# A tower over all pairs of 32 embeddings: split pair kernels streamed per half batch, against plain ones kept on chip in four stages

## What is computed

```python
p = emb_inputs[:, ROW]; q = emb_inputs[:, COL]          # 496 pairs
kp = jnp.einsum('bpj,ipj->bpi', p, kernel)              # kernel (64, 496, 64)
z = jnp.sum(kp * q, axis=-1)
h = jnp.concatenate([z, dense_ctx], axis=1)
h = jnp.maximum(h @ W_top1 + b_top1, 0.0)
h = jnp.maximum(h @ W_top2 + b_top2, 0.0)
y = h @ W_top3
```

## Time and profile before

| | us |
|---|---|
| runs | 574.8, 575.55, 579.02 (median 575.55) |
| the profiled execution | span 578.3; of the runs only 579.02 can hold it, 0.7 more |
| TensorE busy | 479.2 (83%) |
| VectorE busy | 368.1 (64%) |
| ScalarE busy | 120.6 (21%) |
| GpSimd (POOL) busy | 241.3 (42%) |
| DMA | 114.69 MB, mean 198 GB/s |

### The profile page before, as it was taken

How to read it: one execution, slowest core, us unless ns; L and a number is a source line. 1 busy time by engine, 2 the same in 40 slices (tenths; PEclk the granted TensorE clock), 3 DMA queues, 4 the chain that set the end, 5 groups by cost and what they waited for, 6 DMA issues and landing times.

```text
span 578.3 us, 6972 instructions
## 1 busy us (share of the span) xinstructions
PE 479.2 (83%) x2258; PEld 249.9 (43%) x2258; DVE 368.1 (64%) x361; ACT 120.6 (21%) x170; POOL 241.3 (42%) x243
## 2 busy tenths in 40 slices
PE   0568697888988979488998698689889889889998
PEld 0345353444444434244543354435444444445543
DVE  3667584667776855576730387576858787777720
ACT  3275212020121120011043140211212112011002
POOL 3887777776415514050057777764531000000000
PEclk9969897999898989798999799898989999998999
DMA  6768999999999899798886879999999989788600
GB/s 182 184 152 202 241 236 225 213 221 222 229 232 224 191 226 242 174 228 194 198 206 171 177 183 237 204 220 208 224 232 236 230 208 228 194 217 198 139 1 1
DMA packets 43927, 114.69 MB, mean 198 GB/s; under 512 B 9183, under 2 KB 9183, under 8 KB 43758
## 3 DMA queue, kind: packets, MB, share of 16 engines
q1 hardware_dynamic: 36136, 105.91, 78.8%
q0 software_dynamic: 7488, 7.75, 6.2%
q10 hardware_dynamic: 262, 0.52, 0.3%
HBM read 29.72 MB, written 0.00 MB: 51 GB/s over the span
## 4 chain that ended last, share of the span: by engine, by line
DMA 51%; SPq 26%; PE 17%; issue 4%; ACT 1%; DVE 0%; DVEq 0%; ACTq 0%
DMA kst<-ksplit 48%; SPq L290 17%; PE kp L672 6%; SPq L298 3%; PE kp L746 3%; DMA ksplit<-in_kd 3%; PE z_ps L689 3%; PE kp L754 2%; SPq L274 2%; SPq L317 1%; PE kp L715 1%; PE tr_ps L643 1%; DMA own<-split 1%; PE kp L760 1%; SPq L265 0%
## 5 line engine op out<-in xcount | busy, mean ns | idle before, releaser
L620 DVE TENSOR_TENSOR prod<-kp,pair 128x1024 f32<-128x1024 f32 x248 | 292.4, 1219 | 119.8 <-PE kp L672 119.5
L672 PE MATMUL kp<-own,kst 128*128 128x512 f32 x992 | 276.7, 423 | 62.4 <-DMA kst<-ksplit 49.2
L394 POOL DMA_INDIRECT raw<-in_tbl,ids_sb x232 | 239.0, 1030 | 190.8 <-PE tr_ps L643 106.0
L672 PEld LDWEIGHTS kp<-own,kst 128*128 128x128 f32 x992 | 186.4, 198 | 188.1 <-DVE prod L620 75.6
L689 PE MATMUL z_ps<-prod,ones_sel 128*32 128x512 f32 x992 | 139.2, 633 | 0.7 <-DVE prod L620 0.6
L438 ACT ACTIVATE ksplit<-ksplit 128x1024 fp32r<-128x1024 f32 x32 | 33.9, 1059 | 174.6 <-DMA ksplit<-in_kd 174.3
L443 ACT ACTIVATE pair<-tr_ps 128x512 f32<-128x512 f32 x29 | 17.3, 597 | 141.0 <-PE tr_ps L643 141.0
L558 DVE TENSOR_TENSOR ksplit<-ksplit 128x1024 fp32r<-128x1024 f32 x32 | 38.9, 1216 | 9.2 <-ACT ksplit L438 9.1
L564 DVE TENSOR_TENSOR split<-pair,split 128x512 fp32r<-128x512 f32 x29 | 20.2, 697 | 36.3 <-ACT split L447 35.9
L689 PEld LDWEIGHTS z_ps<-prod,ones_sel 128*32 128x32 f32 x992 | 20.1, 110 | 48.9 <-issue 39.2
L715 PE MATMUL kp<-own 125*128 125x512 f32 x48 | 16.6, 502 | 15.4 <-DVE own L592 15.0
(11 more groups left out here) (29 smaller groups left out, 50.3 us busy)
## 6 DMA issues: line engine op xcount, KB each, us to landing
kst<-ksplit SPq DMA_DIRECT2D x128, 512.0 KB
ksplit<-in_kd SPq DMA_DIRECT2D x32, 512.0 KB, 4.1
own<-split SPq DMA_DIRECT2D x116, 128.0 KB
raw<-in_tbl,ids_sb POOLq DMA_INDIRECT x232
pair<-pair SPq DMA_DIRECT2D x16, 128.0 KB
pair<-in_first_ids SPq DMA_DIRECT2D x6, 256.0 KB, 11.3
w_sb<-in_w SPq DMA_DIRECT2D x1, 1024.0 KB, 10.5
pair<-in_tbl SPq DMA_DIRECT2D x4, 250.0 KB
```

Of the source, the lines that this page charges most:

```text
L394: nc.gpsimd.indirect_dma_start(raw[:, k % RAW_RING, b, n, :], None, tables[f], bass.IndirectOffsetOnAxis(ap=ids_sb[:, col:col + 1], axis=0 ...
L620: nc.vector.tensor_tensor(prod[:, s % P_RING, :, :], kp[s % KP_RING][:, :, :], factor, ALU.mult).then_inc(prod_done, 1)
L672: last = nc.tensor.matmul(kp[s % KP_RING][:, q, :], kst[:, c % K_RING, part, t % 2, (t % CHUNK) // 2, :], own[:, o, :], start=(part == 0), ...
```

## The change

K stays unsplit and whole on the chip (`k_sb`, 124 slots x 128 x 128), loaded once during the first stage. The batch is taken in four stages of 256 rows. In a slot the owner of one tile is an even field and that of the other an odd one, so that the two products take rows 0 to 63 and 64 to 127 of the same `pair` place and of `k_sb`; each is a plain fp32 matmul over 64 rows x 256 columns, into its own PSUM bank. `own`, `split`, `kst` and `ksplit` are gone. A *unit* is two slots: 128 x 1024 numbers, 62 a stage, 248 in all. `prod` is a ring of 15 units.

Reductions come in batches of eight units (four in stage 0; the rest of a chunk is 6 or 2), behind the last but one unit of the next batch. Between two reductions lies a *run*. In each run of stages 1 to 3 ScalarE copies the second and the fourth unit's `kp` to `prod` (48 units in all, `SPILLED`); VectorE multiplies those in place, after the other units of the run. 24 units have more than one factor place and are multiplied by two instructions.

Groups are transposed in events: one group each in stage 0 and the first six of stage 1, then two. An event directly behind reductions (`by_halves`) is transposed in halves of 64 rows into the `kp` tile of a unit one or two ahead, which waits for the copy out. Gathers run `RAW_LEAD` = 5 groups ahead, the second of a two-group event also waits for a unit (`PACE`). A group has 256 rows, so four DMAs; 61 groups are gathered. The lookup by comparison stays for three groups of stage 0, in plain fp32. Nine matmuls on zeros stand at TensorE's start. All layers come at the end; the layers' weights are loaded into the places of K's first 24 slots. Everything is unrolled.

```diff
-KP_RING = 3 ... P_RING = 4 ... RAW_RING = 4 ... K_RING = 2 ... AHEAD = 4
+K_LOAD = 8
+K_AHEAD = 3
+KP_RING = 3
+PROD_RING = 15
+RAW_RING = 8
+RAW_LEAD = 5
+WIDTH = 256
+STAGES = ((1,) * GROUPS, (1,) * 6 + (2,) * 5, (2,) * 8, (2,) * 8)
+LAST = len(STAGES) - 1
+STAGES_PER_HALF = ROWS // WIDTH
+BATCH_UNITS = (8,) * 4
+FIRST_BATCH_UNITS = (4,) * 8
+LOOKUP = (0, 1, 2)
+SMALL, SMALL_C = 1000, 8
+HOT_PAUSE = 4
+HOT_UNITS = 2 * SMALL_C * WIDTH // (2 * ROWS)
+WARM = 9
+SPILL_AT = (1, 3)
+PACE = 6
+def summed_behind(b):
+    st, first, n = BATCHES[b + 1]
+    return first + (n - 2 if n % 4 == 0 else n - 1)
+def runs():
+    out = [[]]
+    for u in range(UNITS):
+        out[-1].append(u)
+        if BATCH_OF[u] and u == summed_behind(BATCH_OF[u] - 1):
+            out.append([])
+    return out
+def spilled_units():
+    return [run[i] for run in runs()[1:-1] for i in SPILL_AT if i + KP_RING < len(run)]
+SPILLED = spilled_units()
+DVE_ORDER = [u for run in runs() for u in [u for u in run if u not in SPILLED] + [u for u in run if u in SPILLED]]
 ...
+TRANSPOSE_AT = [0, 0, 0, 1, 2, 4, 7, 10, 13, 16, 19, 23, 27, 31, 35, 39, 43, 47, 51, 55, 59, 62, 65, 69, 77, 85, 93,
+                101, 109, 117, 124, 131, 139, 147, 155, 163, 171, 179, 186, 193, 201, 209, 217]
+def release_event(r):
+    return EVENT_OF[r - RAW_LEAD] if r >= RAW_LEAD else None
+def gather_unit(r):
+    e = release_event(r)
+    return TRANSPOSE_AT[e] + PACE if e is not None and release_event(r - 1) == e else 0
+def by_halves(e):
+    return len(EVENT[e][3]) > 0 and sums_before(TRANSPOSE_AT[e])
+def home_unit(e):
+    return TRANSPOSE_AT[e] + EVENT[e][2]
 ...
         def _(sp):
 ...
+            for u in range(UNITS):
+                st, s = UNIT[u]
+                for m in fours_at(u):
+                    mix_across(st, m)
+                if u == DENSE_AT:
+                    sp.wait_ge(kp_done, u + 1)
+                    sp.dma_start(z_sb[:, FC - 2:FC, :], dense).then_inc(dense_in, 16)
+                if st == 0 and s in K_LOAD_AT and K_LOAD_AT[s] + K_AHEAD < len(K_LOADS):
+                    sp.wait_ge(kp_done, u + 1)
+                    load_k(K_LOAD_AT[s] + K_AHEAD)
+                if st == LAST and s == W_SLOTS:
+                    sp.wait_ge(kp_done, u)
+                    sp.dma_start(w1_sb, w1).then_inc(weights_in, 16)
+                    sp.dma_start(w2_sb, w2).then_inc(weights_in, 16)
 ...
-            def gather(h, k):
 ...
+            for r, (g, b) in enumerate(GATHER):
+                if b and not GATHER[r - 1][1]:
+                    pool.wait_ge(ids_rest_in, 16)
+                if r >= RAW_LEAD:
+                    pool.wait_ge(transposed, release_event(r) + 1)
+                if gather_unit(r):
+                    pool.wait_ge(kp_done, gather_unit(r))
+                for i in range(2):
+                    for n in range(2):
+                        f = 2 * g + n
+                        nc.gpsimd.indirect_dma_start(
+                            raw[:, r % RAW_RING, i, n, :], None, tables[f],
+                            bass.IndirectOffsetOnAxis(ap=ids_sb[:, 2 * b + i, f:f + 1], axis=0),
+                        ).then_inc(raw_in[r % RAW_RING], 16)
         def _(act):
 ...
+            def evacuate(e):
+                st, k, n, raws = EVENT[e]
+                if st >= 2 and k == 0:
+                    act.wait_ge(prod_done, done_through(unit_at(st - 1, 0)))
+                act.wait_ge(transposed, e + 1)
+                to = pair[:, group_place(st, k):group_place(st, k) + n, :]
+                if by_halves(e):
+                    nc.scalar.activation(to.rearrange("p n w -> p (n w)").rearrange("p (m h c) -> p m h c", h=2, c=64),
+                                         halves_ps(e)[:, :, 0:2 * n * 64].rearrange("p h (m c) -> p m h c", c=64),
+                                         ACT.Copy).then_inc(evacuated, 1)
+                else:
+                    nc.scalar.activation(to, event_ps(e)[:, 0:n * WIDTH].rearrange("p (n w) -> p n w", n=n),
+                                         ACT.Copy).then_inc(evacuated, 1)
+            def spill(u):
+                act.wait_ge(reduced, BATCH_OF[u - PROD_RING] + 1)
+                act.wait_ge(kp_done, u + 1)
+                nc.scalar.activation(prod[:, u % PROD_RING, :, :], kp[u % KP_RING][:, :, :],
+                                     ACT.Copy).then_inc(spilled, 1)
 ...
         def _(dve):
 ...
+            def make_hot(i):
+                dve.wait_ge(hot_ids_in[i], 16)
+                for c in range(SMALL_C):
+                    if (i or c) and c % HOT_PAUSE == 0:
+                        dve.wait_ge(hot_ready, SMALL_C * i + c)
+                    nc.vector.tensor_scalar(hot(i, c), hot_ids_sb[:, i, :], row_sb[:, c:c + 1], None,
+                                            ALU.is_equal).then_inc(hot_ready, 1)
+            for u in DVE_ORDER:
+                if u >= PROD_RING and BATCH_OF[u - PROD_RING] >= summed:
+                    summed = BATCH_OF[u - PROD_RING] + 1
+                    dve.wait_ge(reduced, summed)
+                tiles = [tile for x in unit_slots(u) for tile in SLOT[x]]
+                if u in SPILLED:
+                    dve.wait_ge(spilled, SPILLED.index(u) + 1)
+                    columns = prod[:, u % PROD_RING, :, :]
+                else:
+                    dve.wait_ge(kp_done, u + 1)
+                    columns = kp[u % KP_RING]
+                if len({factor_place(st, tile) for tile in tiles}) == 1:
+                    wait_factors(st, tiles[:1])
+                    place = factor_place(st, tiles[0])
+                    nc.vector.tensor_tensor(
+                        prod[:, u % PROD_RING, :, :].rearrange("p q (i n) -> p (q i) n", i=UNIT_SLOTS),
+                        columns[:, :, :].rearrange("p q (i n) -> p (q i) n", i=UNIT_SLOTS),
+                        pair[:, place:place + 1, :].broadcast_to([P, 2 * UNIT_SLOTS, WIDTH]),
+                        ALU.mult).then_inc(prod_done, 1)
 ...
-                    for part in range(2):
-                        last = nc.tensor.matmul(kp[s % KP_RING][:, q, :],
-                                                kst[:, c % K_RING, part, t % 2, (t % CHUNK) // 2, :],
-                                                own[:, o, :], start=(part == 0), stop=(part == 1))
+            def transpose_event(e):
+                st, k, n, raws = EVENT[e]
+                if by_halves(e):
+                    pe.wait_ge(prod_done, DONE_AT[home_unit(e) - KP_RING])
+                elif e > 1:
+                    pe.wait_ge(evacuated, e if e > 2 else 1)
 ...
+                    pe.wait_ge(raw_in[r % RAW_RING], (r // RAW_RING + 1) * 4 * 16)
+                    for i in range(2):
+                        rows = raw[:, r % RAW_RING, i, :, :].rearrange("p a n -> p (a n)")
+                        if by_halves(e):
+                            to = ((g - k) * 2 + i) * 64
+                            for h in range(2):
+                                half = slice(64 * h, 64 * h + 64)
+                                last = nc.tensor.transpose(halves_ps(e)[:, h, to:to + 64], rows[half, :],
+                                                           ident[half, half])
+                        else:
+                            to = (g - k) * WIDTH + i * P
+                            last = nc.tensor.transpose(event_ps(e)[:, to:to + P], rows, ident[:, :])
+                last.then_inc(transposed, 1)
+            def products(u):
+                st, s = UNIT[u]
+                if u - KP_RING in SPILLED:
+                    pe.wait_ge(spilled, SPILLED.index(u - KP_RING) + 1)
+                elif u >= KP_RING:
+                    pe.wait_ge(prod_done, DONE_AT[u - KP_RING])
+                for e in range(len(EVENT)):
+                    if by_halves(e) and home_unit(e) == u:
+                        pe.wait_ge(evacuated, e + 1)
+                for i, x in enumerate(unit_slots(u)):
+                    if st == 0 and x in K_LOAD_AT:
+                        pe.wait_ge(k_in[K_LOAD_AT[x]], 16)
+                    for q in range(2):
+                        owner = SLOT[x][q][0]
+                        rows = slice(64 * q, 64 * q + 64)
+                        pe.wait_ge(evacuated, group_event(st, owner // 2) + 1)
+                        last = nc.tensor.matmul(kp[u % KP_RING][:, q, i * WIDTH:(i + 1) * WIDTH], k_sb[rows, x, :],
+                                                pair[rows, group_place(st, owner // 2), :],
+                                                start=True, stop=True)
+                last.then_inc(kp_done, 1)
+            def reductions(b):
+                st, first, n = BATCHES[b]
+                tiles = batch_tiles(b)
+                c = tiles[0][0] // CHUNK_UNITS
+                if tiles[0][0] == 0 and st:
+                    pe.wait_ge(z_last, st)
+                elif tiles[0][0] and tiles[0][0] % CHUNK_UNITS == 0:
```

(85 more changed lines are left out.)

832 lines of the change are left out of this document (308 added, 524 removed).

## The result

The changed kernel takes 427.03 us (426.82 to 428.68), the kernel before on the same chip 575.37: a ratio of 0.739 (0.734 to 0.744). The profiled execution spans 425.0 us, against 578.3. I had said 444, between 410 and 495. In all ratios and medians here, executions over 1.5% longer than the fastest of the same kernel in their group are left out.

What follows compares the result with a forecast made beforehand. It took the DMA stall of K's split and spread transfers as the bound, about 97 us of the loops, with TensorE's order beneath. Stage 0's 126 us plus 272 made 398; layers 43.2 and 3 gave 444 us, range 410 to 495.

Steps and rivals of the forecast that it cites:

- the column quarters: Old reductions: eight records take 1.00 us, not 3.44, so tiles run side by side; hence 0.90 us a product unit.
- Start: Before the first unit: comparisons end at 19.7 us, then lookup, evacuation and latencies; unit 0 at about 22 us.
- Stage 0: First stage: gathers hold unit 23 until about 64 us, then 39 units at 1.59 us, ending at 126 us.
- the run of four: First stage: next transposes wait for the last unit's multiplication, so the cycle is 6.35 us, 1.59 a unit.
- Stages 1 to 3: After the first stage: 186 units at 1.46 us, in runs of eight of 11.7 us, take 272 us.
- The walk through a run: Run of eight: copies and multiplications come before the units that need them; VectorE is hidden with 2.5 us to spare.
- Later 10 us of gathers per 11.7 us run are hidden: After stage 0: gathers, released some ten units ahead, are hidden behind the runs.
- The end: After the last unit: layers 43.2 us, all at the end, and 3 us from there to the span's end.
- 1: Every product: row halves do not run together, 1.72 us a unit instead of 0.90, +203 us, 647; chance 0.10.
- 2: Products: loads don't hide within a half, 1.28 us a unit, +94 us, 538; chance 0.08.
- 3: TensorE's records start slower or halves overlap partly (1.05 us a unit, +37, 481), gathers lag, or clock halves; chance 0.16.
- 4: Stage 0 waits for each load of K: 16 loads x 4.1, +66 us, 510; chance 0.04.

Runs made afterwards that it cites:

- half_gathers: Changed kernel with only the even field of each group gathered in stage 0, odd fields left zero: 415.93 us.
- q_outer: Changed kernel with a unit's four matmuls reordered, both slots' lower rows first, then both slots' upper rows: 422.76 us.
- four_lookups: Changed kernel with a fourth group of stage 0 looked up by comparison instead of gathered: 418.58 us.
- k_reload: Changed kernel with K loaded anew in every stage, by the same loads three ahead: 423.15 us.
- fours: Changed kernel with batches and runs of four in all stages, so without ScalarE's copies: 432.69 us.

## Why the prediction was right, by its steps

The bound was read rightly: the loops stood under the spreading of K, 83 us in them by experiment for the 97 derived. So was the mechanism that carried the sum, the row halves in parallel, taken from the column quarters; 0.863 us a unit for 0.90. 444 was 17 us too high; in the span, 19.2 (444.2 against 425.0), which fall on these terms:

- **Start, -4.3.** Unit 0 at 17.7 us, not 22. The comparisons started 4.1 us earlier than I had said, and only 0.9 us passed from their end to unit 0, not 2.3; against that, each took 0.46 us and not 0.40 (+1.2 in all). I had carried a DMA's landing time over from the earlier trace rows although the loads around it had changed. Which of them made the difference, no run shows: in both kernels one load stands ahead of row_sb in SyncE's queue. From the changed kernel's timeline:

```profile
5.79 11.02 DVE L582 TENSOR_SCALAR prod<-hot_ids_sb,row_sb 128x512 f32<-128x512 int32 x24 [5.79 <-DMA row_sb<-in_row_no]
5.84 1.09 POOL L478 DMA_INDIRECT raw<-in_tbl,ids_sb  x1 [4.79 <-DMA ids_sb<-in_ids]
...
17.66 1.14 PE L685 MATMUL kp<-pair,k_sb 64*128 64x256 f32 x8
```

- **Stage 0, -9.0** (95.0 us for 104). From unit 23 on it is -6.4, and the step that failed is the run of four: "the next transposes wait for the last unit's multiplication", 6.35 us. It mistook the place: a group's half transposes go into the ring place of the unit after next, so they wait for the last but one, and nothing waits. The changed kernel's timeline gives 5.63 us:

```profile
96.47 0.34 PE L662 MATMUL kp<-ident,raw 64*128 64x64 f32 x4
96.64 3.67 PE L685 MATMUL kp<-pair,k_sb 64*128 64x256 f32 x32
100.25 1.92 PE L703 MATMUL z_ps<-prod,ones_sel 128*32 128x512 f32 x16
102.10 0.34 PE L662 MATMUL kp<-ident,raw 64*128 64x64 f32 x4
```

  The other -2.6 lie before unit 23, which came at 57.1 us for 64: POOL had begun at 5.84, not 10.36. The gathers' hold was there; stage 0 is 95.0 - 15.5 x 5.63 = 7.7 us above its undisturbed runs, and half_gathers gave back 4.2 of such a stage.
- **Stages 1 to 3, -12.4** (259.6 for 272). A run is 10.93 us, not 11.7: transposes 0.3 instead of 0.8, products 6.9 instead of 7.2, reductions as said (3.64 with the last one's end). The waits of the next item and the lower clock behind them stand against that: half_gathers, where TensorE never waits for rows, needs 7.6 us less from unit 62 to the last product record (251.8 for 259.4). The walk through a run held: the copies are in time, and VectorE pauses 0.5 us here and there.
- **"Later 10 us of gathers per 11.7 us run are hidden" was wrong in size.** POOL starts one gather per 1.25 us, and from 5.84 to 147 us it hardly pauses (longest distance 1.70 us): runs of 10.93 leave it 0.9 us each to catch up, so the backlog of stage 0 shows at the beginning of stage 1. From 147 to 288 us it pauses for 0.8 to 1.1 us in most runs, and yet rows are late at the beginning of every later stage: TensorE's waits for them are 1.51 us, ending at 123.51, 0.67 at 210.92, 0.96 at 296.95 and 2.38 at 310.48. The last gather starts at 325.2. From the changed kernel's timeline, POOL first, then TensorE:

```profile
308.58 0.94 POOL L478 DMA_INDIRECT raw<-in_tbl,ids_sb  x1 [0.30 <-issue]
309.83 0.95 POOL L478 DMA_INDIRECT raw<-in_tbl,ids_sb  x1 [0.30 <-issue]
```

```profile
307.76 0.34 PE L662 MATMUL kp<-ident,raw 64*128 64x64 f32 x4
310.48 0.34 PE L662 MATMUL kp<-ident,raw 64*128 64x64 f32 x4 [2.38 <-DMA raw<-in_tbl,ids_sb]
310.65 8.81 PE L685 MATMUL kp<-pair,k_sb 64*128 64x256 f32 x64
319.39 3.64 PE L703 MATMUL z_ps<-prod,ones_sel 128*32 128x512 f32 x32
```

  Taking gathers away gave 7.4 us, replacing four 4.8.
- **The end, +6.5.** From the last unit on 52.7 us, not 46.2: two batches of reductions (3.6 and 2.7 us) still come behind it. I had them in the units' price, so this term moved between stretches and is no error of the sum.

The rivals: 1 would have been slower by what it said (+202 us measured for +203), but the halves do pair. 2 (loads don't hide within a half) did not come: 64 loads run in 6.79 us under 64 matmuls in 7.13, and with all products in one row half they stayed hidden too: 64 loads in 13.69 us under 64 matmuls in 14.03, 0.22 each. What lets a load go ahead there, no run shows. 3 kept two parts, both small: the gathers, and the clock, which was halved three times in the changed kernel (granted 0.50 or 0.51 from 24.6 to 28.0, 123.6 to 127.0 and 311.3 to 314.8 us), each time right behind a wait for rows (ended at 24.59, 123.51 and 310.48). 4 is refuted twice, by the page, whose chain has no load of K, and by reloading K. The 1.65 us in the prediction's run of four stand there without a row of their own; what the trace shows in their place is a run of 5.63 us that doesn't wait for VectorE. The 500 in the range's "500 to 510 as a rest" has no run behind it either; the changed kernel and its variants that compute the whole took 418.58 to 440.54 us.

## What to carry to other kernels

A contraction over 64 rows in plain fp32, put in pairs on the two halves of the rows, cost no more array time than the same product split into two fp32r parts over 128 rows (0.863 us a unit here, 1.02 a slot before, from 2.04 for two in the earlier trace rows), and needed neither the splitting nor a second copy: look for such layouts where a profile's chain is made of rearranging. When an engine's average slack seems to cover another's phase, compare their rates inside that phase and count the ring's places; two copies of eight were worth 1 us a run here. And add up each queue's own work against the whole span: 244 gathers of 1.25 us from 5.8 us on come to 311, and the last ended at 326: these 15 us of pauses were all the slack there was.

## What the runs showed of the hardware that I had not expected

- Two matmuls in different row halves overlap also when they aren't neighbours in the queue (records at 201.146 and 201.151 us in q_outer), for 0.1 us more a run.
- Transposes of 64 x 64 in pairs: eight records in 0.29 us until the next product, 0.037 each, so the loads of two row halves overlap too, each being a record of 0.14 us that starts 3 to 4 ns beside its partner's; I had taken 0.105, from the earlier trace rows.
- A wait of 2.4 us on TensorE cost more than itself: the 64 products behind it took 8.81 us instead of 7.13, with the granted clock at 0.81 in that stretch, that is partly at half the full clock (0.51 from 311.3 to 314.8 us). The row of a stretch before it and of that one:

```profile
297.10:304.20 7.10, 7.10 (x70) 5.92 (x68) 5.56 (x7) 3.58 (x5) 5.56 (x6) 1.00 0.37 84
310.60:319.40 8.80, 8.80 (x69) 7.18 (x69) 4.92 (x5) 3.69 (x5) 6.67 (x8) 0.81 0.14 26
```

  In half_gathers and four_lookups, where no rows were waited for after the start, the clock stayed at 1.00. It did so too in k_reload and fours, with waits for rows of up to 1.5 and 1.8 us, so such a wait doesn't always bring it down.
